# A pair's transposed scores ahead of the next utterance's scores

## The reference

```
scores = einsum('bhqd,bhkd->bhqk', q, k) * scale        # per head and utterance
scores = where(causal, scores, -inf)                    # the first three attentions
probs  = softmax(scores, axis=-1)
out    = einsum('bhqk,bhkd->bhqd', probs, v)            # then a projection, added to h
```

## Time and profile before

| what | value |
|---|---|
| time, median of 3 runs | 4184.95 us (4178.12 to 4190.71) |
| time of the profiled execution | 4172.62 us |
| its span, from the first to the last instruction | 4170.9 us |
| PE busy | 3284.4 us (79%), 23447 instructions |
| DVE busy | 2086.2 us (50%) |
| ACT busy | 1232.1 us (30%) |
| POOL busy | 1221.4 us (29%) |
| mean granted clock of PE over the span | 0.853 |

### The profile page before, as it was taken

One profiled execution on the slowest core, in us unless ns is written; L12 is line 12 of the kernel. 1 busy time (PEld: TensorE's weight loads), 2 busy tenths in 40 slices (PEclk: granted clock), 3 DMA queues, 4 the chain that ended last, 5 costly groups with the idle time before them and its releaser, 6 DMA issues. The chain is left out here.

```text
span 4170.9 us, 70241 instructions
## 1 busy us (share of the span) xinstructions
PE 3284.4 (79%) x23447; PEld 2210.8 (53%) x23448; DVE 2086.2 (50%) x4029; ACT 1232.1 (30%) x2459; POOL 1221.4 (29%) x934
## 2 busy tenths in 40 slices
PE   7589981649997699999606996478888887579999
PEld 3357761326775367777505995234334333256777
DVE  0444437323445245555542333478888888731443
ACT  2222110011121122222213442265555565413222
POOL 0102110102120124334171002656556555510221
PEclk9698875778888899999658998689888888769998
DMA  1000000570000200000241112222212221100000
GB/s 46 12 1 0 0 2 11 88 97 1 0 0 11 88 1 0 0 0 0 70 137 50 45 50 60 74 58 54 52 46 58 52 52 52 36 10 0 9 11 10
DMA packets 250482, 140.02 MB, mean 34 GB/s; under 512 B 175329, under 2 KB 226467, under 8 KB 250384
## 3 DMA queue, kind: packets, MB, share of 16 engines
q1 hardware_dynamic: 230480, 122.61, 12.0%
q0 software_dynamic: 18432, 12.40, 1.3%
q10 hardware_dynamic: 1472, 3.85, 0.3%
HBM read 103.41 MB, written 35.21 MB: 33 GB/s over the span
## 5 line engine op out<-in xcount | busy, mean ns | idle before, releaser
L2414 DVE TENSOR_TENSOR_SCAN ssm_state<-ssm_dA,ssm_dBx 128x372 f32<-128x372 f32 x512 | 434.3, 910 | 103.3 <-ACT ssm_dA L2203 82.6
L2109 POOL TENSOR_TENSOR ssm_dBx<-ssm_du,ssm_bc_wide 128x1488 f32<-128x1488 f32 x128 | 426.9, 3340 | 196.5 <-DVE ssm_state L2414 195.1
L2288 PE MATMUL ssm_y<-ssm_hC,top_ident 128*128 128x512 f32 (+1 forms) x768 | 405.9, 671 | 93.8 <-DVE ssm_hC L2419 86.6
L2203 ACT ACTIVATE ssm_dA<-ssm_delta,ssm_decay 128x368 f32<-128x368 f32 x512 | 276.7, 565 | 190.9 <-DVE ssm_state L2414 179.2
L2288 PEld LDWEIGHTS ssm_y<-ssm_hC,top_ident 128*128 128x128 f32 x768 | 157.6, 216 | 307.9 <-issue 165.2
L2419 DVE TENSOR_TENSOR ssm_hC<-ssm_state,ssm_c_wide 128x1488 f32<-128x1488 f32 x128 | 218.1, 1704 | 5.1
L643 ACT ACTIVATE dattn_probs<-dattn_scoresT 93x372 f32<-93x372 f32 x256 | 108.1, 472 | 350.9 <-PE dattn_scoresT L556 350.9
L570 PE MATMUL dattn_outputs<-dattn_v,dattn_probs 93*93 (+1 forms) x2048 | 185.4, 233 | 0.0
L570 PEld LDWEIGHTS dattn_outputs<-dattn_v,dattn_probs 93*93 93x93 f32 x2048 | 181.8, 163 | 3.4
L489 POOL TENSOR_TENSOR rattn_q<-rattn_q_all,rattn_only 128x372 f32<-128x372 f32 x64 | 51.7, 807 | 439.6 <-PE rattn_scoresT L556 247.2
L1409 POOL TENSOR_TENSOR dattn_square<-dattn_square,top_minus_half 93x16 f32<-93x16 f32 x32 | 92.7, 2896 | 271.9 <-DVEq L1485 271.9
(11 more groups left out here) (546 smaller groups left out, 7209.1 us busy)
## 6 DMA issues: line engine op xcount, KB each, us to landing
ssm_bc_wide<-bc_rows SPq DMA_DIRECT2D x128, 372.0 KB, 4.3
route_stage<-in_L_ffn_W SPq DMA_DIRECT2D x32, 512.0 KB, 4.2
qkv_rows<-rattn_rows SPq DMA_DIRECT2D x32, 288.0 KB, 3.1
rattn_heads<-qkv_rows SPq DMA_DIRECT2D x96, 96.0 KB, 3.5
moe_sent<-top_blank SPq DMA_DIRECT2D x1, 7936.0 KB, 23.6
tiles_x_in<-moe_sent SPq DMA_DIRECT2D x31, 256.0 KB, 2.8
moe_back<-tiles_y SPq DMA_DIRECT2D x31, 256.0 KB, 2.1
tok_frames<-in_frames ACTq DMA_DIRECT2D x8, 376.0 KB, 8.4
```

What stands on the lines that cost most here:

```text
L2109: pool.tensor_tensor(dBx[:, k % 2, :, :], du[:, :, :], bc_wide[:, q % BUFS, 0, k % 2, :].unsqueeze(1).broadcast_to([P, CC, GT]), ALU.mult) ...
L2203: act.activation(by_utterance(dA[:, ring(k, c), 0:GT])[:, :, 1:], by_utterance(delta[:, c, :])[:, :, 1:], ACT.Exp, scale=decay[:, c, k:k + ...
L2288: mm = pe.matmul(ps_y[:, at], ident[:, :], hC[:, k % 2, :, :].rearrange("p c t -> p (c t)")[:, at], start=(k == 0), stop=(k == N - 1), ski ...
L2414: dve.tensor_tensor_scan(state[:, k % 2, c, :], dA[:, ring(k, c), 0:GT], dBx[:, k % 2, c, :], 0.0, ALU.mult, ALU.add).then_inc(scanned, 1)
```

## The change

In `utterance` one call moves: `scores_t(b, buf, p)` now stands ahead of `scores(b + 1, 1 - buf, p)` and `turn_ctx(b - 1, ..)`. Nothing else changes: each engine issues the same instructions with the same waits, and only PE's order differs.

```
     def utterance(b, buf, first, last, second=False):
         pairs = a.units // 2
         for p in range(pairs):
+            scores_t(b, buf, p)
             if not last:
                 scores(b + 1, 1 - buf, p)
             if p == pairs - 1 and not first:
                 turn_ctx(b - 1, 1 - buf, second)
-            scores_t(b, buf, p)
             if p:
                 weigh(b, buf, 2 * p - 2)
                 weigh(b, buf, 2 * p - 1)
```

## The result

The kernel after took 4203.28 us (median of 4 runs, 4201.67 to 4215.55), the kernel before beside it 4184.66 us: 18.6 us more, a ratio of 1.0052 with a 95% interval of 1.0040 to 1.0064. So it is slower by more than the 0.3% that can be told from no change.

A forecast was written before the change was run, and what follows sets the result against it. PE's order bounds all four attentions, then the granted clock. Full clock: gattn -2.5, rattn -2.5, dattn +9.0, eattn +2.5, sum +6.5; clock -2; total +4.5 on 4184.95 gives 4189 us, range 4163 to 4211.

The forecast's parts named there:

- the term of the clock: Granted clock over the stages: -5 us each in gattn and rattn, +8 in dattn, -2 us in all.
- what the new neighbours cost: In dattn, changed neighbours on PE add 0.44 us per utterance, less 0.15 for C's saved wait: +0.29.
- Neighbours in gattn and rattn: New piece neighbours on PE save 0.08 us per utterance, 2.5 us in each stage; M to T taken as no difference.
- The clock of gattn and rattn: -5 us in each stage, near no change, since the stretch ahead of the clock's falls stays; bounds -42 or -46 to +16.
- the list of waits that can take over: Five places, (a) to (e), where another wait might come last; only eattn's second T was to wait, 0.23 us.
- (e): DVE gets its maxima one T X (1.1 us) later and POOL's cuts are released earlier; both cost 0.
- C's wait: In dattn C waits 0.15 us for the context; after the move PE comes later, so the wait goes.
- The clock of dattn: +8 us, half of the 16 it pays, since four more drains stand around its W W; bounds -16 to +53.
- The other covers: No wait at pair 0's X for the `maxT` copy (0.48 us cover) or last W W for exponentials (0.46).
- The slower rival: dattn's clock falls oftener around W W, mean grant 0.93, losing 37 us instead of 16: +28, 4213 us; chance 0.25.
- The faster rival: Clock falls in gattn and rattn come half as often: -30 us in all, 4155 us; chance 0.20.
- The late `maxT` copy: Pair 0's X waits for the copy, its cover gone by 0.2 us each utterance: +25, 4214 us; chance 0.05.

The follow-up runs named there:

- e2: Against the kernel before, the new order in gattn and rattn alone, dattn and eattn keeping the old one: 4195.97 us, ratio 1.0023.
- e12: The new order in gattn and rattn alone, against the kernel before, run and profiled a second time unaltered: 4187.25 us, ratio 1.0002.
- e7: Against the kernel after, in dattn DVE takes pair 0's context ahead of its maxima and POOL the cut ahead of the power: 4200.85 us, ratio 1.0052.
- e8: Against the kernel before, in gattn and rattn alone the last pair's turn_ctx and next scores stand between the two W W: 4149.57 us, ratio 0.9924.
- e6: Against the kernel before, POOL takes the cut for the utterance after the next ahead of the power (concerns dattn alone): 4184.39 us, ratio 0.9997.
- e3: Against the kernel after, in dattn DVE takes the context part of pair 0 ahead of pair 0's maxima: 4260.09 us, ratio 1.0186.
- e9: Against the kernel after, M of gattn and rattn held until the last product with v, the addition ahead of the split: 4206.84 us, ratio 1.0067.

## Why the prediction was right or wrong

The range held the time because it was wide; the forecast's sum was 13.5 us short of the four loops. Against the second profile of the kernel before, gattn was forecast at -2.5 - 5 = -7.5 us and came out at +0.7, rattn at -7.5 and at -3.2, dattn at 9 + 8 = +17 and at +17.6, eattn at +2.5 and at +2.9. So nearly all of the miss lies in gattn and rattn, in the term of the clock: taken as a gain of 5 us each, it was a loss that took back more than the neighbours were forecast to give. That dattn's total agrees is luck: a wait of 7.4 us was missing from it, and what the new neighbours cost (0.29 taken for 0.22 an utterance, 2.2 us) and the clock (8 for 3.3 us) were put too high.

- **Neighbours in gattn and rattn: right in direction, too small.** C to W W measured 0.22 (0.23 taken). M to T took 0.13 where M to A took 0.22, and W W to P 1.27 for 1.31; the first I had put at no change, the second I had not listed. The 0.19 for M to T was read wrongly: in the earlier trace rows M is two products, in gattn one. In dattn M to T did take 0.19 (1755.74 to 1755.93). The utterance lost 0.24 us at full clock, three times the 0.08. An utterance of gattn in the kernel after, on PE, with the copy to `maxT` on DVE:

```profile
404.15 0.20 PE L540 MATMUL gattn_general<-top_ident,gattn_split 93*32 93x93 bf16 x1
404.28 0.87 PE L549 MATMUL gattn_scoresT<-gattn_q,gattn_k 64*93 64x372 f32 x4
404.49 0.20 DVE L680 COPY gattn_maxT<-gattn_general 32x93 bf16<-32x93 bf16 x1 [0.49 <-PE gattn_general L540]
...
405.08 0.55 PE L556 MATMUL gattn_scoresT<-gattn_maxT,gattn_sel 128*93 128x93 bf16 x8
...
409.13 0.38 PE L581 MATMUL gattn_general<-top_ident,gattn_ctx 93*128 93x93 f32 x2
409.35 1.42 PE L570 MATMUL gattn_outputs<-gattn_v,gattn_probs 93*93 x16
410.62 1.08 PE L593 MATMUL gattn_general<-gattn_w_out,gattn_ctxT 128*93 128x256 f32 x4
411.53 1.43 PE L570 MATMUL gattn_outputs<-gattn_v,gattn_probs 93*93 x16
412.94 0.24 PE L540 MATMUL gattn_general<-top_ident,gattn_split 93*32 93x93 bf16 x1
```

- **The clock of gattn and rattn: wrong, and the step that failed in the total.** I took -5 each, "near no change, since the stretch ahead of the falls stays". It did stay, the falls go on beginning in the last W W (before, every second one began in M right behind it), and they are as many, but longer: once the pattern repeats, each lasts 6.8 us, where before every second one lasted 3.4. Before, the lengths of four utterances repeat as 9.04, 9.47, 10.40 and 12.05 us, 40.96 in all; after, two repeat as 11.46 and 9.02, 20.48. Both make 10.24 us per utterance, so the 0.24 us saved at full clock went to the clock whole. In e2 and e12, with the same order, gattn's and rattn's loops are within 1.1 us of the kernel before. Why the two means agree so closely is open. The grant of 0.84 lies outside the 0.85 to 0.91 that I had named as proof against me.
- **dattn: the list of waits that can take over was not whole.** For `weigh` it considered the exponential alone and left out `outputs_read` (L562), and (e) put DVE's delay of one T X at nothing. The move takes T X of pair 0 out from between pair 0's S and the first W W, and there the context of the utterance before must still be read by DVE. It costs 0.24 x 31 = 7.4 us. Without that wait (e7) the utterance is longer by 0.22 us, where +0.29 was predicted, with S to W W 0.83 and W W to T 1.42 (0.83 and 1.39 named). C's wait went as said. At full clock dattn's loop grew by 0.46 x 31 = 14.3 us, where the sum had 9.0.
- **The clock of dattn: small, as taken, but not readable from one profile.** +8 was taken; against the second profile 17.6 - 14.3 = 3.3 us are left for it (41 us at 1.2 GHz in place of 38). My bound of 0.94 was not passed (0.95). The base was off: the 16 us that I read as dattn's loss belonged to one short execution, and its second profile has a grant of 0.96 in place of 0.97.
- **eattn: right.** T of the second pair waits for the exponentials, 0.17 us where 0.23 was expected, and the utterance grew by 0.08, as the sum had it:

```profile
4024.59 0.55 PE L556 MATMUL eattn_scoresT<-eattn_maxT,eattn_sel 128*93 128x93 bf16 x8
4025.07 0.90 PE L530 MATMUL eattn_scores<-eattn_k,eattn_q 64*93 64x93 f32 x16
4025.08 0.85 ACT L643 ACTIVATE eattn_probs<-eattn_scoresT 93x372 f32<-93x372 f32 x2 [2.76 <-PE eattn_scoresT L556]
...
4025.97 0.24 PEld L549 LDWEIGHTS eattn_scoresT<-eattn_q,eattn_k 64*93 64x93 f32 x4 [0.17 <-ACT eattn_probs L643]
```

- **The other covers held.** X of pair 0 came 0.80 behind T with no wait (copy ended at 404.69, X started at 405.08: 0.39 of cover for the 0.48 named). The last W W followed P in 0.91 (0.92 before) and did not wait for exponentials.
- **The rivals.** The slower rival named the place, dattn, and its time, 4213, was nearer than the forecast's 4189. Its price was wrong: it laid 21 us to the clock, and the runs show 14.3 us at full clock, half of it a wait, and 3.3 us of clock. The faster rival, fewer falls in gattn and rattn, is a real way for this kernel, but by another order (e8). The late `maxT` copy did not come: its cover was there.

## What to carry to other kernels

When a piece moves on an in-order engine, list for every piece that now comes sooner all the waits written in it, those of first units too, and time each releaser on its own engine; the wait that bites may be one that never showed. Where the granted clock falls again and again in a stage, as here, a gain at full clock need not be a gain of the stage: read the mean over a whole repeat of falls, and try where the falls begin. Set each stage's forecast beside its own measurement, since a sum can agree, or miss, for another reason than the one that was found. And one profile of each kernel can differ by more than the effect: profile the kernel before twice before a stage that the edit does not touch is blamed.

## What the runs showed of the hardware that was not expected

- Two-input DVE instructions of 0.42 us took 1.62 to 1.65 us beside one POOL cut of 1.44 us, and 3.25 beside two cuts in a row (the kernel before, e6 and e3), so here the order of POOL sets DVE's times.
- A pause of 0.34 us per utterance cut gattn's time at 1.2 GHz by 22 us without making the falls fewer (e9), and another order of the same pieces, with a pause of 0.31 us, made them half as many (e8).
- The same program had 24 or 38 us at 1.2 GHz in one loop, in two profiled executions of the kernel before, perhaps on different chips, while its gattn and rattn loops repeated within 0.6 us.
